# Edge passes of a graph network: destination rows and one-hots in float32, one matmul per tile instead of three bfloat16 parts

## The reference

```
m   = maximum(concat(x[src], x[dst], edge) @ W1 + b1, 0) @ W2 + b2      # layer 0
x   = layernorm(x + segment_sum(m, dst))
g   = leaky_relu(xl[src] + xr[dst] + edge @ W_e)                        # layer 1
out = segment_sum(xl[src] * softmax_over_dst(g . att), dst)
x   = layernorm(x + gelu(batchnorm(out) + x))
# layer 2: a one-head softmax layer, layer 3: a mean over the neighbours
```

## Time and profile before

| | |
|---|---|
| median of 3 runs | 6610.97 us (6607.07 to 6613.7) |
| the profiled execution | 6620.37 us, its span 6618.7 us |
| mean granted TensorE clock | 0.630 of full speed |
| busy | PE 4926.0 us (74%), PEld 3702.2 us (56%), DVE 3854.6 us (58%), ACT 1920.7 us (29%), POOL 4014.0 us (61%) |
| mlp pass | about 81 to 2650 us of the span |
| gatv2 pass | about 2797 to 5220 us of the span |

### The profile page before, as it was taken

The page is one execution under the profiler, slowest core; times in us unless marked ns, Lnnn a source line. Parts: engine busy times, 40 slices in busy tenths (PEclk is TensorE's granted clock), DMA queues, the critical chain, the costliest instruction groups (busy, mean ns, idle before and its releaser), DMA issues. The chain is left out here.

```text
span 6618.7 us, 104783 instructions
## 1 busy us (share of the span) xinstructions
PE 4926.0 (74%) x33518; PEld 3702.2 (56%) x33518; DVE 3854.6 (58%) x7688; ACT 1920.7 (29%) x4445; POOL 4014.0 (61%) x4125
## 2 busy tenths in 40 slices
PE   5566777777777776467777777777776469999689
PEld 4455666766667765356666566666655332222289
DVE  3122355555555542356666666666665469999855
ACT  1111222222222211112222222222211149999811
POOL 4555566666666665366666666666666627787634
PEclk6555566565565555555555555555555579999899
DMA  6644355555555544244444444444444334343298
GB/s 164 113 111 132 103 150 150 148 144 146 145 149 149 148 136 116 65 118 130 132 132 131 131 127 130 132 131 131 131 131 115 72 101 129 124 129 124 69 336 301
DMA packets 897045, 902.75 MB, mean 136 GB/s; under 512 B 635824, under 2 KB 779480, under 8 KB 880373
## 3 DMA queue, kind: packets, MB, share of 16 engines
q1 hardware_dynamic: 568404, 708.29, 33.9%
q0 software_dynamic: 115488, 115.45, 9.0%
q10 hardware_dynamic: 212608, 72.31, 4.8%
HBM read 656.88 MB, written 239.54 MB: 135 GB/s over the span
## 5 line engine op out<-in xcount | busy, mean ns | idle before, releaser
L507 POOL DMA_INDIRECT mlp_G<-mlp_src,src_cols x1612 | 1531.3, 950 | 1027.5 <-PE mlp_z L873 480.7
L507 POOL DMA_INDIRECT gatv_G<-gatv_src,src_cols x1612 | 1529.2, 949 | 940.1 <-DMA X<-in_x 435.7
L691 DVE TENSOR_TENSOR mlp_hots<-mlp_in_psum,src_lo 128x1024 bf16<-128x1024 bf16 x608 | 416.6, 685 | 734.3 <-remote 573.7
L909 PE MATMUL gatv_sums<-gatv_msg,gatv_same 128*128 128x68 f32 x3234 | 712.0, 390 | 151.7 <-issue 149.8
L909 PEld LDWEIGHTS gatv_sums<-gatv_msg,gatv_same 128*128 128x128 f32 x3234 | 688.2, 310 | 171.2 <-issue 169.1
L909 PE MATMUL mlp_sums<-mlp_zs,mlp_same 128*128 128x64 f32 x3234 | 676.5, 389 | 64.8 <-issue 64.6
L909 PEld LDWEIGHTS mlp_sums<-mlp_zs,mlp_same 128*128 128x128 f32 x3234 | 648.4, 301 | 66.0 <-issue 65.9
L2201 POOL TENSOR_TENSOR keys<-src_lo,gsoft_ring 128x512 f32<-128x512 f32 (+1 forms) x448 | 505.1, 1133 | 182.5 <-ACT src_lo L2344 172.7
L2266 PE MATMUL gsoft_acc<-keys,masks 128*64 128x512 f32 (+1 forms) x1568 | 558.2, 621 | 77.0 <-DVE keys L2440 42.1
L869 PE MATMUL gatv_z<-attr_w,gatv_attrT 112*128 112x448 f32 x462 | 422.3, 1017 | 206.3 <-DVE gatv_msg L597 107.9
L873 PE MATMUL mlp_z<-mlp_win,mlp_hot 128*128 128x64 bf16 x4851 | 384.6, 232 | 240.2 <-issue 236.2
(11 more groups left out here) (481 smaller groups left out, 8498.5 us busy)
## 6 DMA issues: line engine op xcount, KB each, us to landing
mean_block<-blocks SPq DMA_DIRECT2D x62, 1568.0 KB
gsoft_ring<-blocks SPq DMA_DIRECT2D x105, 896.0 KB
sums_gatv<-gatv_out_rows SPq DMA_DIRECT2D x231, 252.0 KB
mlp_rel<-rel_rows SPq DMA_DIRECT2D x116, 448.0 KB
gatv_rel<-rel_rows SPq DMA_DIRECT2D x116, 448.0 KB
sums_mlp<-mlp_out_rows SPq DMA_DIRECT2D x231, 224.0 KB
blocks<-masks SPq DMA_DIRECT2D x31, 1568.0 KB
blocks<-work SPq DMA_DIRECT2D x31, 1568.0 KB
```

The costliest lines, as they stand in the source:

```text
L507: pool.indirect_dma_start(out=G[:, b.gq, j * L.gathered:(j + 1) * L.gathered], out_offset=None, in_=L.gather_table, in_offset=bass.Indirec ...
L691: last = nc.vector.tensor_tensor(hot_of[:, slot(b, k), :, :, :], bc(steps2_of[:, 0:w, :], 1, [P, OCTET // K2, w, K2]), bc(of_step[:, cols] ...
L909: last = pe.matmul(sums[b.q % 2][:, j * L.msg:(j + 1) * L.msg], same[:, b.q, j, :], rhs, start=True, stop=True)
```

## The change

For the layers with windows the destination table is stored in float32, as it comes out of the projection, in rows of 256 bytes instead of 384. The roundings and subtractions of `Tables` go. `win` is float32 with 64 columns, `hot` is float32 too, with three slots (`HOTS`) in place of four, and each tile takes one float32 matmul in place of three bfloat16 ones. The one-hots are compared from bfloat16 inputs into a float32 output, in the way in which `same` is.

```diff
-            hot = sb("hot", [P, Q, B, P], L.win_dt)
-            win = sb("win", [P, Q, B, L.parts * L.window], L.win_dt)
+            hot = sb("hot", [P, HOTS, B, P])
+            win = sb("win", [P, Q, B, L.window])
...
-                wait(dve, z_made, b.used(Q))
-                if L.win_dt == BF16:
-                    nc.vector.tensor_tensor(
-                        hot[:, b.q, :, :].rearrange("p b (a e) -> p (b a) e", e=D // 2),
-                        rel[:, b.q, :].rearrange("p (b e) -> p b e", e=D // 2), bc(lanes_of, 1, [P, 4 * B, D // 2]),
-                        ALU.is_equal
-                    ).then_inc(hot_made, 1)
-                else:
-                    nc.vector.tensor_tensor(hot[:, b.q, :, :], relv[:, b.q, :, :],
-                                            bc(lane_of, 2, [P, B, P]), ALU.is_equal).then_inc(hot_made, 1)
+                wait(dve, z_made, b.used(HOTS))
+                nc.vector.tensor_tensor(hot[:, b.hot, :, :], relv[:, b.q, :, :],
+                                        bc(lane_of, 2, [P, B, P]), ALU.is_equal).then_inc(hot_made, 1)
...
-                        for part in range(L.parts):
-                            last = pe.matmul(z[b.q % 2][:, j * w:(j + 1) * w], hot[:, b.q, j, :],
-                                             win[:, b.q, j, part * w:(part + 1) * w],
-                                             start=not ax and part == 0, stop=True, skip_group_check=True)
+                        last = pe.matmul(z[b.q % 2][:, j * w:(j + 1) * w], hot[:, b.hot, j, :], win[:, b.q, j, :],
+                                         start=not ax, stop=True, skip_group_check=True)
...
-        if L.parts == 3:
-            g, w = L.gathered, L.window
-            left = self.table[:, q, 0:m0, g:g + w]
-            for part in range(2):
-                out = left if part == 0 else self.parts[:, q, 0:m0, 2 * w:3 * w]
-                dve.wait_ge(self.rounded, 2 * c + part + 1)
-                v.tensor_tensor(out, left, self.parts[:, q, 0:m0, part * w:(part + 1) * w], ALU.subtract
-                                ).then_inc(self.left, 1)
...
-            eng.dma_start(node_view(L.window_table)[:, k0:k0 + m0, :], self.parts[:, q, 0:m0, :]
+            eng.dma_start(node_view(L.window_table)[:, k0:k0 + m0, :], self.table[:, q, 0:m0, g:g + w]
...
-        Layer(0, "mlp", D, D, 32, 0, dram("mlp_src", [NP, D]), dram("mlp_dst", [NP, 3 * D], BF16)),
-        Layer(1, "gatv2", D, D, 16, HEADS, dram("gatv2_src", [NP, D]), dram("gatv2_dst", [NP, 3 * D], BF16)),
+        Layer(0, "mlp", D, D, 32, 0, dram("mlp_src", [NP, D]), dram("mlp_dst", [NP, D])),
+        Layer(1, "gatv2", D, D, 16, HEADS, dram("gatv2_src", [NP, D]), dram("gatv2_dst", [NP, D])),
```

More of the change, by code:

```diff
@@ L33 @@
 GQ = 8
+HOTS = 3
 FOUR = 4
@@ L91, in __init__ @@
         self.row = D + 2 * heads
-        self.parts = 3 if window == D else 1
-        self.win_dt = BF16 if self.parts == 3 else F32
 def in_slot(slot):
@@ L108, in __init__ @@
         self.q = c % Q
+        self.hot = c % HOTS
         self.n = loop * U + c
@@ L1291, in tables @@
                     projection.on_scalar(act, projection.numbers("table", c))
-                    if c > chunks[0]:
-                        made.on_scalar(act, c - 1)
-                made.on_scalar(act, chunks[-1])
             act.wait_ge(edges_in, 16 * 6)
@@ L1469, in __init__ @@
         self.stores = 2
-        if L.parts == 3:
-            self.parts = ctx.enter_context(nc.sbuf_tensor(n + "_parts", [P, 2, CHUNK, 3 * L.window], BF16))
-            self.rounded = ctx.enter_context(nc.semaphore(n + "_rounded"))
-            self.left = ctx.enter_context(nc.semaphore(n + "_left"))
     def on_vector(self, dve, c):
@@ L1488, in on_vector @@
         dve.sem_inc(self.filled, 1)
-        if L.parts == 3:
-            g, w = L.gathered, L.window
-            left = self.table[:, q, 0:m0, g:g + w]
-            for part in range(2):
-                out = left if part == 0 else self.parts[:, q, 0:m0, 2 * w:3 * w]
-                dve.wait_ge(self.rounded, 2 * c + part + 1)
-                v.tensor_tensor(out, left, self.parts[:, q, 0:m0, part * w:(part + 1) * w], ALU.subtract
-                                ).then_inc(self.left, 1)
-    def on_scalar(self, act, c):
-        L, q = self.L, c % 2
-        if L.parts != 3:
-            return
-        m0, g, w = CHUNKS[c][1], L.gathered, L.window
-        act.wait_ge(self.filled, c + 1)
-        wait(act, self.stored[q], 16 * self.stores * (c // 2))
-        for part in range(2):
-            if part:
-                act.wait_ge(self.left, 2 * c + 1)
-            act.activation(self.parts[:, q, 0:m0, part * w:(part + 1) * w], self.table[:, q, 0:m0, g:g + w],
-                           ACT.Copy).then_inc(self.rounded, 1)
     def store(self, eng, c):
@@ L1517, in store @@
                      ).then_inc(self.stored[q], 16)
-        if L.parts == 3:
-            eng.wait_ge(self.left, 2 * (c + 1))
-            eng.dma_start(node_view(L.window_table)[:, k0:k0 + m0, :], self.parts[:, q, 0:m0, :]
+        with self.nc.allow_non_contiguous_dma(reason="rows of the window table"):
+            eng.dma_start(node_view(L.window_table)[:, k0:k0 + m0, :], self.table[:, q, 0:m0, g:g + w]
                          ).then_inc(self.stored[q], 16)
-        else:
-            with self.nc.allow_non_contiguous_dma(reason="a column of the window table"):
-                eng.dma_start(node_view(L.window_table)[:, k0:k0 + m0, :], self.table[:, q, 0:m0, g:g + w]
-                             ).then_inc(self.stored[q], 16)
     def all_stored(self, sp):
@@ L1817, in _ @@
                     projection.on_scalar(act, projection.numbers("w2", c))
-                if made and c - 2 >= 0:
+                if L.name == "gatv2" and c - 2 >= 0:
                     made.on_scalar(act, c - 2)
```

## The result

The changed kernel takes 6814.75 us (median of 6 runs, 6808.35 to 6846.96), the kernel before 6610.96 us (6607.07 to 6635.1): 1.0311 times as long, 95% interval 1.0294 to 1.0327. The direction was forecast, the size was not: 3.1% against 8.5%, and the time lies under the range. The profiled execution took 6846.96 us with a span of 6845.2 us, 226.5 us more than the span before; it is the longest of the six, so the medians differ by less, 204 us.

A forecast was written before the change was run, and what follows sets the result against it. TensorE's loop was taken to lead in mlp with builds, with loop and gathers near one another in gatv2. 6620.4 + 320 (mlp) + 246 (gatv2) - 7 (tables) = 7179, less 9: 7170 us, 8.5% slower; range 6880 to 7500.

The forecast's parts named there:

- The price of z on TensorE: Both edge passes: float32 matmuls for bfloat16 ones, +1.86 us per batch at the lower clock, weighted +1.67 mlp, +1.80 gatv2.
- Mlp with builds: Mlp pass, batches 48 to 199: TensorE's loop leads, so the full price of z counts, 152 x 1.67 = 254 us.
- The first 48 and the last 31 batches: Mlp pass, start and end: half the price of z charged, 40 us and 26 us.
- Gatv2 with builds: Gatv2 pass, 192 batches: middle between pauses as slack and pauses as real, 1.28 us each, 246 us, from 146 to 346.
- The break of GpSimd: Gatv2 pass: GpSimd idles 1.95 and 1.92 us ahead of each batch, read as waiting until earlier gathers have landed.
- One-hots on VectorE: Both edge passes: longer comparison, +0.47 us per batch, counted 0 because VectorE has free time; without that cover up to 162 us.
- Windows: Window loads of both edge passes: 256 bytes per row for 384, no gain counted.
- Tables: Dense stages: two copies and two subtractions per chunk go, -7 us in all.
- hide the gatv2 part: Rival, gatv2 pass: pauses and hand-off shrink, the pace stays at the gathers' 10.4 us per batch; 6924 us, chance 0.14.
- that rival: Rival, both edge passes: float32 z takes away TensorE's upper clock level, +336 us on top, 7506 us; chance 0.17.
- the cheap matmul: Rival, z on TensorE: float32 matmul at four bfloat16 steps, 220 ns per tile, +0.39 us per batch; 6715 us, chance 0.04.

The follow-up runs named there:

- bf_six: The kernel before with each bfloat16 matmul of z made twice, 42 per batch: 1.0568 times the kernel before of its group.
- bf_one_part: The kernel before with 7 of the 21 bfloat16 matmuls of z per batch, all parts still loaded: ratio 0.9959 to the kernel before.
- f32_wide: The changed kernel with 384-byte rows in the mlp pass's window loads, gatv2 as changed: 7116 us, 1.0594 times the kernel before.
- bf_hots_long: The kernel before with the one-hots of z compared tile by tile, seven VectorE instructions for one: ratio 1.0141 to the kernel before.
- bf_narrow: The kernel before with window loads of 256 bytes per row for 384, TensorE's work as before: ratio 0.9997 to the kernel before.
- bf_no_rel: The kernel before with the loads of rel left out from the fifth batch on: ratio 0.9951 to the kernel before at 5766.4 us.
- bf_no_windows: The kernel before with window loads left out from the fifth batch of each edge pass on: ratio 0.9917 to the kernel before at 5766.4 us.
- f32_no_gathers: The changed kernel with gathers left out from the ninth batch of both edge passes on: 5909 us, ratio 0.8806 to the kernel before.
- after_again: The changed kernel, unedited, run again beside the kernel before at 5766.4 us: ratio 1.0715.
- bf_no_gathers: The kernel before with gathers left out from the ninth batch of both edge passes on: 5203 us, ratio 0.9023 to the kernel before.

## Why the prediction was wrong

Of the 226.5 us of span, 2.3 were won before the first add and 73.1 lost in the mlp pass (90.8 to 2714.4 against 93.1 to 2643.6), 1.8 lost between the passes, 152.7 in gatv2, 1.2 behind it.

- *The price of z on TensorE* was right at the lower clock level: 216 ns per record, 3.02 us per batch. In gatv2 TensorE is busy 1.81 us longer per batch, where +1.80 was forecast. In mlp it is 1.22 for 1.67: the three parts had not taken 1.16 us there. Their group shows 250.9 us of busy time, 1.66 per batch, and 1.0 more of idle inside.
- *Mlp with builds* is the step that failed: "TensorE's loop leads, all of it counts: 152 x 1.67 = 254 us". It cost 0.32 us x 151 = 48. Work of 1.22 us came and idle time of 0.91 went. I had read the pauses in L873 and let them stand in the sum as if they were fixed, while in gatv2 I asked whether they were slack. The lower bound of 254 had no reason; there were 1.91 us of pauses per batch, more than the price, and with the question put there too the bound would have been near zero. That gathers wait for z does not show whose loop z stands in. The claim that TensorE's loop leads is half true: `bf_six` paid 1.19 us for 1.16, `bf_one_part` got back 0.16 for 0.77.
- *The first 48 and the last 31 batches* of mlp, 40 and 26 us forecast: 13.05 to 13.40 us per batch over the first 48, 17 us, and about 9 for the last.
- *Gatv2 with builds*, 246 us forecast, 146 as the lower bound with pauses as slack: 0.83 x 191 = 159 us. The answer was near the lower bound, and taking the middle was the error: z's stretch grew by the full price, and the pauses inside the sums went. That 11.24 us fit the 11.18 of that bound is partly luck: the bound took away one pause of 0.57 us, the trace keeps 0.96 us per batch among the builds, and in the long condition of `f32_wide` the same pass took 11.92. Without builds the period was 10.24, for 10.4 forecast. The break of GpSimd, read as a wait until gathers have landed, stands in no wait of the program, so the 10.4 us were no floor of the gathers as such.
- *One-hots on VectorE*: 1078 ns as forecast. Nothing in gatv2, rightly. In mlp the sum put them at nothing because VectorE has 5 us free per batch, and that reason failed: `bf_hots_long` paid 0.37 us for 0.39. At that rate the 0.47 us would cost 0.44 us per batch, an estimate, more than the 0.32 that the whole change cost there. So those 0.32 us may be VectorE's price, with TensorE's all taken up by pauses, or a part of each; no run has the float32 z without the longer comparison.
- *Windows* with a third less: nothing, rightly (`bf_narrow`). *Tables*, -7 us: next to nothing, -2.3 and +1.8.
- *The rivals.* The gathers do not hide the gatv2 part; GpSimd waits for z. They hide the mlp part, and only in the short condition (8.5 to 8.7 us with float32 z, 8.5 in the kernel before without rel or windows, of which there is no unedited trace in that condition; the loops alone 6.81 and 6.25). The clock fell to 0.50 in gatv2, the lower level throughout, as that rival had it there; in mlp it kept 0.58 of 0.60, so the larger half of the 336 us did not come. A float32 tile takes 3.02 / 7 = 0.431 us, eight steps of 55 ns and not four, so the cheap matmul is out. The Trainium skill speaks of four passes for true FP32 ("FP8 and Floating Point Precision", TensorE Precision Notes); read as four bfloat16 steps, that gave 6715 us, an estimate, and the trace does not agree with this reading. That the time came out between it and my sum is no evidence for it.

What stands shown: in the short condition, with no pauses, the change costs gatv2 1.9 to 2.0 us per batch beside `bf_no_rel` and `bf_no_windows`, the 1.86 of the lower clock level in full and a little more (the clock is at 0.57 and 0.62 in those two and at 0.50 in the changed kernel), and the whole kernel 7.1%. Where there are pauses (1.9 to 2.9 us of "issue" per batch before TensorE's matmuls in the kernel before, 0.9 to 1.1 in the changed one in the first measurement), they moved or shrank when TensorE's work changed, and the price showed in part. How large a part depends on the group: 3.1% at 6611 us, 5.9% at 6716 with the wider windows of `f32_wide`, 7.1% at 5766. So the 3.1% is itself a number of one condition.

What stays open: why TensorE's idle time shrank by 0.9 to 1.0 us with float32 z in the first trace but grew with twice the bfloat16 matmuls (2.36 to 3.31 in gatv2); which engine's added work the mlp pass paid for; and what the two conditions are. Gathers are needed for the pauses, windows' bytes are not their cause, the rate of the gathers is not. Whether window or rel transfers take part was not seen in the long condition.

## What to carry to other kernels

An idle time that the trace puts down to nothing ("issue") is a term of the sum with two ends, zero and full, in every stage alike; a bound that is argued in one stage and forgotten in the next is where a sum goes wrong. An engine that is free for half of its time on average can still stand in the loop of a stage: lengthen its instruction alone, as `bf_hots_long` does, before its price is set to nothing. Measure the kernel before again beside each experiment, and if its own time falls by 14%, ask which resource sets the pace in each of the two cases before carrying a ratio over. For a float32 matmul of 128x64 with fresh weights count two records of 216 ns at the lower clock level, as measured here, beside 55 ns for each bfloat16 part; two parts in place of three saved 0.5% where it was run.

## What the hardware showed unasked

- The same kernel took 6711 to 6716 or 5766 to 5778 us, depending on the group; chips 8 and 11 showed the first, chips 5, 7 and 8 the second. GpSimd's gathers took 0.94 us each in both. The kernel before had, in the first of them, a break of about 2 us ahead of each batch's gathers of gatv2 that no wait of the program explains, and pauses of the other engines; the short condition has neither, and without gathers the pauses are gone too (`f32_no_gathers`).
- TensorE's granted clock in the mlp pass was higher where the pace was: 0.60 at 10.8 us per batch (kernel before), 0.70 at 8.6 (`after_again`), 0.93 at 6.25 (`bf_no_gathers`). With float32 z in gatv2 it stayed at 0.50, the lower level, with TensorE busy 91% of the time (1890.8 of 2070.9 us, `after_again`).
- A comparison of 128x128 elements took 213 ns, seven of them in a row 1.00 us, and one of seven times as many elements 0.61.
